# Tokens turned by half-array matmuls, a gate of 14 steps with its bias on GpSimd and its division on ScalarE, and a new order of the last stage

## The reference

```python
x = x + conv_sweeps(_ln_c(x), w_d, w_u, w_r, w_l)
t = _to_tokens(x)
n = _ln_t(t)
router_probs = softmax(n @ router_w + router_b)        # 8 experts
top_p, top_i = top_k(router_probs, 2)
top_p = top_p / sum(top_p)
expert_out = einsum('bnd,edc->bnec', n, expert_w) + expert_b
t = t + einsum('bnk,bnkc->bnc', top_p, gathered(expert_out, top_i))
```

## Time and profile before

| | |
|---|---|
| median of 3 runs | 1264.97 us (1264.68 to 1266.33) |
| the profiled execution | 1265.12 us, its span 1263.3 us |
| expert stage, from its first gate | 877.78 to the end |
| busy over the span | PE 99%, PEld 91%, DVE 59%, ACT 42%, POOL 42% |
| DVE in the last ten of 40 slices | 9 tenths or more in nine of them |

### The profile page before, as it was taken

One profiled execution on the slowest core, in us unless ns is written; L12 is line 12 of the kernel. 1 busy time (PEld: TensorE's weight loads), 2 busy tenths in 40 slices (PEclk: granted clock), 3 DMA queues, 4 the chain that ended last, 5 costly groups with the idle time before them and its releaser, 6 DMA issues.

```text
span 1263.3 us, 30783 instructions
## 1 busy us (share of the span) xinstructions
PE 1251.2 (99%) x11007; PEld 1151.7 (91%) x11007; DVE 743.9 (59%) x1614; ACT 531.3 (42%) x1433; POOL 532.0 (42%) x654
## 2 busy tenths in 40 slices
PE   9999999999999999999999999999999999999997
PEld 7999999999999999999999999999777777777776
DVE  5666666555555322222222222344999999999998
ACT  6555555334333322222200000121666767676763
POOL 1555554000000000000024444455887889888886
PEclk9999999999999999999999999999999999999999
DMA  5222222000000000000002212210001010101011
GB/s 165 70 66 71 68 77 74 0 0 1 0 0 0 0 0 0 0 0 0 0 24 70 70 47 70 71 48 25 2 32 76 28 54 27 54 28 54 28 54 54
DMA packets 15837, 47.62 MB, mean 38 GB/s; under 512 B 2961, under 2 KB 3473, under 8 KB 15761
## 3 DMA queue, kind: packets, MB, share of 16 engines
q1 hardware_dynamic: 15616, 46.28, 10.9%
q10 hardware_dynamic: 144, 0.33, 0.1%
HBM read 31.86 MB, written 14.75 MB: 37 GB/s over the span
## 4 chain that ended last, share of the span: by engine, by line
PE 97%; DVE 2%; ACT 1%; issue 0%; POOL 0%; POOLq 0%; DVEq 0%; ACTq 0%
PE twin L1240 36%; PE twin L1104 29%; PE twin L1279 13%; PE twin L1298 7%; PE twin L1213 5%; PE twin L1229 3%; PE twin L1143 2%; PE twin L1124 0%; PE twin L1131 0%; PE twin L1163 0%; DVE act_buf L1057 0%; ACT spare L717 0%; DVE scratch L1049 0%; DVE spare L1049 0%; DVE act_buf L896 0%
## 5 line engine op out<-in xcount | busy, mean ns | idle before, releaser
L1240 PE MATMUL twin<-kbuf,late 128*128 128x136 f32 (+2 forms) x3940 | 457.5, 279 | 0.2 <-ACT kbuf L642 0.2
L1240 PEld LDWEIGHTS twin<-kbuf,late 128*128 128x128 f32 x3940 | 456.4, 191 | 0.4 <-issue 0.4
L1104 PE MATMUL twin<-parts 128*128 128x384 f32 (+2 forms) x2070 | 379.5, 342 | 0.0
L1104 PEld LDWEIGHTS twin<-parts 128*128 128x128 f32 x2070 | 366.8, 188 | 3.0 <-issue 0.4
L1012 DVE SCALAR_TENSOR_TENSOR kbuf<-twin,act_buf 128x144 f32<-128x144 f32 x394 | 121.2, 308 | 329.6 <-PE twin L1240 329.4
L428 POOL TENSOR_TENSOR act_buf<-kbuf,x_in 128x144 f32 (+1 forms) x140 | 68.5, 489 | 516.6 <-DVE kbuf L1012 516.6
L1279 PE MATMUL twin<-em,parts 64*128 64x512 f32 x1350 | 213.8, 421 | 2.5 <-ACT spare L717 1.3
L1279 PEld LDWEIGHTS twin<-em,parts 64*128 64x128 f32 x1350 | 112.0, 187 | 23.6 <-issue 9.5
L665 ACT ACTIVATE act_buf<-kbuf 128x144 f32 x196 | 63.2, 323 | 162.2 <-DVE kbuf L1012 162.1
L680 ACT ACTIVATE squares<-twin 128x384 f32<-128x384 f32 (+1 forms) x81 | 37.9, 468 | 209.8 <-PE twin L1213 207.3
L817 DVE SCALAR_TENSOR_TENSOR act_buf<-twin,act_buf 128x400 f32 (+1 forms) x70 | 40.2, 574 | 72.9 <-PE twin L1104 51.0
(11 more groups left out here) (128 smaller groups left out, 1578.8 us busy)
## 6 DMA issues: line engine op xcount, KB each, us to landing
x_in<-x_col SPq DMA_DIRECT2D x20, 720.0 KB, 4.1
result<-act_buf SPq DMA_DIRECT2D x34, 400.0 KB, 3.0
scratch<-x_tok SPq DMA_DIRECT2D x8, 448.0 KB, 3.3
spare<-x_tok SPq DMA_DIRECT2D x8, 448.0 KB, 3.3
scratch<-x_tok SPq DMA_DIRECT2D x8, 384.0 KB, 3.1
spare<-x_tok SPq DMA_DIRECT2D x8, 384.0 KB, 3.1
x_in<-x SPq DMA_DIRECT2D x3, 400.0 KB, 5.3
x_in<-x SPq DMA_DIRECT2D x2, 200.0 KB, 3.8
```

The costliest lines, as they stand in the source:

```text
L1104: last = mm(acc[:, lo:hi], vw[:, k, wpart, si], carry[:, cpart, g, lo + s * BG:hi + s * BG], start=first and si == 0, stop=final and si == ...
L1240: last = mm(banks[CONV[g]][:, lo * BG:hi * BG], hw[:, k, si], kbuf[:, g, lo + s:hi + s].rearrange("p j b -> p (j b)"), start=si == 0, stop ...
```

## The change

- Turning from region 2 on uses two half-array matmuls per tile, one per half of 64 channels, with new weights `cl_h` of 72 columns. They write the banks LOG and CTB, and ScalarE reads both with one square and two copies per chunk. Since LOG is the gate's work space, TensorE waits before a region's first chunk until all steps of the gate in work are done.
- The bias is added by GpSimd, behind the scaling of a region's last chunk, from an SBUF copy of the bias, and counted in s_bl; the gate's first step waits for that.
- The division is ScalarE's: ln(1 + ex), then exp of minus that. The gate has 14 steps. Its last waits for s_iv.
- Tables: fewer tiles are copied (7 and 6 become 5 and 5), three instead of two are scaled in a long region, so five instead of four are whole on VectorE in either kind. All steps move ahead of gate 7, and the turning begins behind them.
- Four small copies more make `cl_h` before the column sweep.

```diff
-        ACT_TILES = [(4, 6), (4, 6)]
-        COPY_TILES = [(0, 1, 2, 5, 10, 11, 12), (0, 1, 2, 5, 10, 11)]
+        ACT_TILES = [(1, 3, 4), (5, 6)]
+        COPY_TILES = [(0, 2, 5, 6, 10), (1, 2, 3, 4, 10)]
...
-        SMN = 17
+        SMN = 14
...
+        SCALE_AT = [[(7, 1), (8, 1), (10, 1), (11, 1), (11, 1)],
+                   [(8, 0), (8, 1), (10, 1), (10, 1)]]
...
# GpSimd, scale_tokens
                 if half != 0:
                     nc.gpsimd.tensor_tensor(xn, xn, inv.to_broadcast([P, k, 2, C]), ALU.mult).then_inc(s_xn2, 1)
+                    if c == NCH[r] - 1:
+                        ng = 2 * NT[r]
+                        pool.wait_ge(s_em, EM_READY)
+                        pool.wait_ge(s_xn2, n + 1)
+                        if r > 0:
+                            pool.wait_ge(s_sm, (r - 1) * SMN + 2)
+                        nc.gpsimd.tensor_tensor(logit[:, 0:ng], raw_logit[:, 0:ng], bias_row[:, :].unsqueeze(1).to_broadcast([P, ng, E]),
+                                                ALU.add).then_inc(s_bl, 1)
...
# ScalarE, copy_tokens from region 2 on, and exponential
+                halves = twin[LOG // 2][:, :, 0:k * HW].rearrange("p q (t n) -> p t q n", n=HW)
+                act.activation(by_half[0], halves[:, :, :, 0:C], ACT.Square).then_inc(s_sq2, 1)
+                act.activation(by_half[1], halves[:, :, :, 0:C], ACT.Copy)
+                act.activation(by_half[2], halves[:, :, :, C:], ACT.Copy).then_inc(s_cp, 1)
...
                 act.activation(best[:, 1], best[:, 0], ACT.Exp).then_inc(s_ex, 1)
+                act.wait_ge(s_ex, r + 1)
+                act.activation(best[:, 3], best[:, 1], ACT.Ln, bias=1.0).then_inc(s_el, 1)
+                act.wait_ge(s_el, r + 1)
+                act.activation(best[:, 2], best[:, 3], ACT.Exp, scale=-1.0).then_inc(s_iv, 1)
...
# VectorE, softmax_steps and softmax
-                    lambda: v.tensor_tensor(lg, raw_logit[:, 0:ng], bias_row.unsqueeze(1).to_broadcast([P, ng, E]), ALU.add),
-                    lambda: v.tensor_scalar(den, ex, 1.0, None, ALU.add),
-                    lambda: v.reciprocal(inv, den),
...
                 if k == 0:
-                    dve.wait_ge(s_xn2, chunk_no(r) + NCH[r])
+                    dve.wait_ge(s_bl, r + 1)
                 elif k == EX_STEP:
                     dve.wait_ge(s_ex, r + 1)
+                elif k == INV_STEP:
+                    dve.wait_ge(s_iv, r + 1)
...
# TensorE, tokens
                 else:
                     pe.wait_ge(s_tl, back_no(r))
+                    pe.wait_ge(s_sm, SMN * r)
...
+                    for q in range(2):
+                        half = slice(q * C, (q + 1) * C)
+                        last = mm(banks[LOG + q][:, HW * k:HW * (k + 1)], tokens_of(r, p, p + 1)[half], cl_h[half, :],
+                                  start=True, stop=True)
```

More of the change, by code:

```diff
@@ L98, in metaformer_kernel @@
         center_w = cl_w[:, 0:P]
+        HW = C + E
+        cl_h = sb("cl_h", [P, HW])
         eps_c = sb("eps_c", [P, 3])
@@ L193, in stored_after @@
             return group_no(last[0]) + last[1] + 1
-        bias_row = banks[LOG][:, 2 * NSM + 3 * NG:2 * NSM + 3 * NG + E]
         def stage_of(n):
@@ new lines, in metaformer_kernel @@
+        GAP_STEP = 7
+        EX_STEP, INV_STEP = 11, 13
+        TURN_AT = [[(7, 1), (9, 0), (9, 2), (11, 1), (12, 2)],
+                   [(7, 1), (8, 1), (9, 2), (10, 2)]]
+        COPY_AT = [[(6, 1), (7, 1), (9, 0), (10, 1), (11, 0)],
+                   [(6, 1), (7, 0), (10, 0), (10, 1)]]
+        VAR_AT = [[(8, 0), (8, 2), (10, 0), (11, 2), (12, 2)],
+                   [(7, 2), (9, 0), (9, 1), (11, 0)]]
+        INV_AT = [[(7, 1), (8, 0), (10, 1), (11, 0), (11, 1)],
+                   [(7, 0), (8, 1), (10, 1), (11, 1)]]
@@ L324, in metaformer_kernel @@
         s_sm = sem("s_sm")
+        s_bl = sem("s_bl")
         s_ex = sem("s_ex")
+        s_el = sem("s_el")
+        s_iv = sem("s_iv")
         s_p = sem("s_p")
@@ L446, in scale_tokens @@
                     if c == 0 and r > 0:
-                        pool.wait_ge(s_sm, (r - 1) * SMN + 1)
+                        pool.wait_ge(s_bl, r)
                     nc.gpsimd.tensor_tensor(lg, xl, inv.to_broadcast([P, k, 2, E]), ALU.mult)
@@ L843, in expert_low @@
                 nc.vector.tensor_tensor(em[:, 1], ew[:, 0:E * C], em[:, 0].bitcast(F32), ALU.subtract).then_inc(s_em, 1)
+                for q in range(2):
+                    half = slice(q * C, (q + 1) * C)
+                    nc.vector.tensor_copy(cl_h[half, 0:C], center_w[half, half]).then_inc(s_em, 1)
+                    nc.vector.tensor_copy(cl_h[half, C:], ew[half, E * C:]).then_inc(s_em, 1)
             last_work = [lambda: low_weights(1), expert_mean, expert_bias, expert_high]
@@ L972, in softmax_steps @@
                 small = banks[LOG][:, 2 * NSM:2 * NSM + 3 * NG].rearrange("p (k n) -> p k n", k=3)[:, :, 0:ng]
-                m1, idx, den = (small[:, k] for k in range(3))
+                m1, idx = (small[:, k] for k in range(2))
                 rank, lg, ht, fi = rank_w[:, 0:ng], logit[:, 0:ng], hit[:, 0:ng], first[:, 0:ng]
                 return [
-                    lambda: v.tensor_tensor(lg, raw_logit[:, 0:ng], bias_row.unsqueeze(1).to_broadcast([P, ng, E]), ALU.add),
                     lambda: v.tensor_reduce(m1, lg, AX.X, ALU.max),
@@ L1212, in tokens @@
                 for k, p in enumerate(tiles_of(c, r)):
-                    last = mm(banks[bank][:, CLW * k:CLW * (k + 1)], tokens_of(r, p, p + 1), cl_w[:, :],
-                              start=True, stop=True)
+                    if r < 2:
+                        last = mm(banks[bank][:, CLW * k:CLW * (k + 1)], tokens_of(r, p, p + 1), cl_w[:, :],
+                                  start=True, stop=True)
+                        continue
+                    for q in range(2):
+                        half = slice(q * C, (q + 1) * C)
+                        last = mm(banks[LOG + q][:, HW * k:HW * (k + 1)], tokens_of(r, p, p + 1)[half], cl_h[half, :],
+                                  start=True, stop=True)
                 last.then_inc(s_ct, 1)
```

47 lines of the change are left out of this document (20 added, 27 removed).

## The result

The changed kernel takes 1277.88 us (1277.41 to 1277.96) beside 1264.83 for the kernel before: ratio 1.010 [1.0087, 1.0113], 13.05 us slower. The forecast was 1270, some 5 us above the kernel before; the direction was right, the size 2.5 times too small. The span of the profiled execution went from 1263.3 to 1275.6 us.

What follows compares the result with a forecast made beforehand. VectorE was taken as the bound, and the new order to close a ring of GpSimd and VectorE work at 43.9 us per pair: +5.8, +1.7 and -2.1 make +5.4 on 1265.1, so 1270 us, range 1261 to 1281.

Steps and rivals of the forecast that it cites:

- What bounds the kernel: In the stage behind the column sweep, VectorE bounds: 41.25 of 42.76 us per pair, 1.5 us of waiting.
- The terms for each engine: Per pair: VectorE -0.1 us, TensorE 4 us and under 1 us less, GpSimd 37.0 to 38.9, ScalarE 2.6 more.
- the cheap end: TensorE's turning of a three-tile chunk: both half arrays run side by side at half the columns, 0.47 us.
- The ring: Gate 7, GpSimd's second half, bias, 14 VectorE steps, next gate 7: 43.1 us per pair, 43.9 with three delays.
- the signs named: First step waits about 1 us for GpSimd, GpSimd unbroken to bias, TensorE waits before first chunk, pair 43-45 us.
- one sign of being wrong: VectorE waiting for TensorE or ScalarE elsewhere than at the first step by more than 1 us per pair.
- The sum: Sixteen regions between gates 7: 8 x 43.9 = 351.2 against 345.40 us, +5.8; with first and last regions +5.4.
- edges: Corrections for the first region (+1.7 us) and the last but one (-2.1 us), added to the sixteen regions.
- The bare ring: Rival: the three delays are covered by waits already counted, 43.1 us per pair, 1264 us; chance 0.20.
- TensorE's relief pays: Rival: GpSimd's second halves cost less, TensorE is no longer late, pair 41.4 us, 1250 us; chance 0.12.
- Serial halves: Rival: TensorE's fp32 half arrays run one behind the other, 1.86 us per chunk, 1283 us; chance 0.08.
- More lateness of ScalarE's kind: Rival: ScalarE's delays add 0.5 us per region, +8, 1278 us; part of the forecast's range, which has 0.60.

Runs made afterwards that it cites:

- old-order runs: Kernel before with the division's addition and reciprocal moved to ScalarE, 1264.80 us; kernel before with a third of the turning left out, 1257.02 us.
- the relieved pair: A pair of regions in the kernel before with a third of the turning left out; that run measured 1257.02 us.

## Why the prediction was right or wrong

**What bounds the kernel: wrong.** The prediction took TensorE's full busy share for an artefact of modelled ends and named VectorE. The old-order runs decide it: VectorE's relief 0, TensorE's 7.8 us. The rows said it already: TensorE had 42.74 of 42.74 us, while after the change the same view does show idle time. That the ends are modelled makes the share inexact, as the relieved pair shows, but not meaningless.

**The terms for each engine: mostly right.** VectorE's busy time per pair went from 41.22 to 41.28 (forecast -0.1). GpSimd's grew by 1.8 (forecast 1.9), ScalarE's by 1.4 (forecast 2.6, too dear). The bias lasts 0.64 and 0.60 us, with 0.13 of waiting ahead of it; 0.60 with its wait was taken. The Trainium skill, "GPSIMD Engine Reference", section 3.1, had made it 0.69 by its ratio of 1.96; here it is 0.64 on GpSimd for 0.35 on VectorE, a ratio of 1.8, so the page was nearer than my 0.54 from a line through two rows. The chunk takes 0.70, between the cheap end 0.47 that was taken and 1.86. TensorE lost 2.5 us a pair, not 4 to 5.

**The ring: right in GpSimd's half, and in length in VectorE's.** Long GpSimd 12.68 (forecast 12.5), short VectorE 10.12 (10.0 and 0.2), short GpSimd 11.31 (10.7 and 0.4), long VectorE 10.12 (9.9 and 0.2): 44.23 for 43.9. GpSimd's half is shown by two runs: less turning leaves it, a second bias adds itself. In VectorE's half three steps fewer change nothing, so that its length comes out with VectorE's sum is in part luck. Of the signs named, GpSimd's unbroken stretch and TensorE's wait before the first chunk are there. The wait at the first step is 0.5 us in short and 0.2 in long regions, not 1 us or more in each. And one sign of being wrong came: VectorE waits 1.6 us a pair for ScalarE's squares, where more than 1 was to count against the ring; the run with less turning shows that these waits are not the loss.

**The sum: the step that failed.** The forecast's +5.8 is "8 x 43.9 = 351.2" set against 345.40; measured is +12.33. The left side is eight *steady* pairs; the right is sixteen regions as they were, four of them slow. Both kernels have these; gate 7 of the first region to that of the fifth, before and after:

```profile
888.12:977.03 88.91, 87.02 (x1063) 66.11 (x1063) 82.52 (x172) 59.68 (x187) 74.29 (x86) 1.00 0.10 39
```

```profile
889.17:980.95 91.78, 82.47 (x1117) 63.80 (x1118) 83.75 (x161) 62.50 (x220) 77.90 (x91) 1.00 0.10 38
```

That is 3.4 and 3.3 us above two steady pairs (85.48 and 88.46). Like against like, the prediction's own numbers give 8 x (43.9 - 42.76) = +9.1, not +5.8, and with its edges 1274. The rest: the ring was 0.33 a pair short, 2.6 us; two long regions were 0.3 and 0.4 longer than the others, 0.6. Sum 3.3 + 2.6 + 0.6 = 6.5, which is 12.3 less 5.8. The edges were +1.05 and -1.09 for +1.7 and -2.1: 0.4 more.

**What the ring leaves out.** The prediction made it of VectorE and GpSimd alone, "whatever TensorE does". The length came out, but the traces show TensorE between the first step and gate 7: behind L989, and behind the pair after the bias. Of the first wait it should have asked what is queued behind the waiting step; the order shows L989 there. The second it had, at 0.2; in the steady long region it is 0.47.

**The rivals.** The bare ring (1264) did not come: every stretch is longer than its bare sum, by 0.1 to 0.6 us. "TensorE's relief pays" was priced from the wrong bound: the relief is there (2.5 us of busy time a pair; in this order the half arrays are worth 5.5 us), but a third of the turning less wins nothing more where GpSimd's stretch sets the pace. Serial halves (1283) did not come. *More lateness of ScalarE's kind* hit the number, 1278, by luck: it asked for 0.5 us more a region, and the steady ring has 0.17; most of the rest is the sum's mistake.

## What to carry to other kernels

Before a period is multiplied and set against a measured stretch, cut the stretch at the same places and take the same kind of period on both sides; four slow regions made nearly half of this forecast's error. An engine that is busy to the last hundredth in a window is the first suspect until a run that relieves it says otherwise, also where its ends are modelled. And where an order makes two engines work one after the other, each at 92 to 99% in its own stretch, add up the stretches: no busy share of the whole shows that loss, and making one engine's work lighter gave little back here. An engine that fills its stretch need not be the one that holds it; leave some of its work out and see. Before a loss is put down to a kernel's queues, read the granted clock of its windows.

## What the hardware showed that was not expected

A VectorE addition of two SBUF operands that takes 0.36 us at the least took 3.13 us in the median beside GpSimd's work, up to 3.48. Each of the 17 long ones ended about 0.2 us after a GpSimd instruction did: twelve after the last of three or more back to back, as in the rows above, so that VectorE was passed over at the ends between them; four got in between two, and one came behind a single instruction. With one operand in PSUM it took 0.35 us in all 18. The Trainium skill, "SBUF — State Buffer", section "Who interferes with whom", states that a VectorE instruction with two SBUF inputs contends with a GpSimd instruction that reads SBUF; the trace agrees. Its sentence on how long the blocking lasts, one whole instruction, is about VectorE's two-port modes; here it was mostly longer. The change moves bias_row to SBUF, and that costs nothing like this as long as the addition is not VectorE's.
